# Masked multi-head attention with a pre-norm: own steps for each chunk of products, q and k halves moved one by one, three-term denominators, no loops

## What is computed

```python
h = jnp.maximum(_layernorm(x, axis=-1), 0.0)
q = heads(h @ Wq + bq); k = heads(h @ Wk + bk); v = heads(h @ Wv + bv)
scores = jnp.einsum('bhqd,bhkd->bhqk', q, k) * scale
scores = jnp.where(mask[:, None] == 0, -jnp.inf, scores)
attn = jax.nn.softmax(scores, axis=-1)
out = jnp.einsum('bhqk,bhkd->bhqd', attn, v)
x = x + out.transpose(0, 2, 1, 3).reshape(b, s, D_MODEL) @ Wo + bo
```

## Time and profile before

| | |
|---|---|
| median of three runs | 2085.54 us (2085.31 to 2088.58) |
| the profiled execution | 2085.51 us |
| its span, first to last instruction | 2083.6 us |
| granted TensorE clock, mean | 0.989 |
| PE busy | 1932.5 us, 93% |
| DVE, ACT, POOL busy | 75%, 71%, 62% |
| chain that ended last, PE's share | 76% |
| PE idle before scores, in wait for a mask | 61.4 us |

### The profile page before, as it was taken

How to read it: one execution, slowest core, us unless ns; L and a number is a source line. 1 busy time by engine, 2 the same in 40 slices (tenths; PEclk the granted TensorE clock), 3 DMA queues, 4 the chain that set the end, 5 groups by cost and what they waited for, 6 DMA issues and landing times.

```text
span 2083.6 us, 40441 instructions
## 1 busy us (share of the span) xinstructions
PE 1932.5 (93%) x14336; PEld 776.5 (37%) x14336; DVE 1557.3 (75%) x1587; ACT 1478.1 (71%) x1765; POOL 1302.1 (62%) x581
## 2 busy tenths in 40 slices
PE   3799899998999999999999999999899998999977
PEld 2334344343344333443334333334333343444312
DVE  5688777878768787687867877778767787767773
ACT  3577786677867788668876778767777677866672
POOL 0377567556666567656667557666557566676574
PEclk8999999999999999999999999999999999999999
DMA  5433244342444324343351434424234332442302
GB/s 177 122 87 96 82 112 132 88 107 64 120 112 124 83 76 132 86 122 86 92 142 56 115 93 117 119 74 119 81 109 122 88 106 66 117 122 64 74 1 81
DMA packets 103222, 206.61 MB, mean 99 GB/s; under 512 B 11616, under 2 KB 11744, under 8 KB 103008
## 3 DMA queue, kind: packets, MB, share of 16 engines
q1 hardware_dynamic: 103008, 203.80, 35.2%
HBM read 153.43 MB, written 50.33 MB: 98 GB/s over the span
## 4 chain that ended last, share of the span: by engine, by line
PE 76%; DVE 7%; issue 6%; DMA 5%; ACT 2%; POOL 1%; SPq 1%; DVEq 0%; ACTq 0%; POOLq 0%
PE ps L694 20%; PE ps L681 19%; PE ps L654 15%; PE ps L705 10%; PE ps L668 7%; PE ps L661 6%; DVE ring L905 4%; DMA k_stack<-k_parts 2%; DMA k_parts<-k_part 1%; SPq L513 1%; DMA edges<-adjT 1%; ACT hT_hi L776 1%; DVE k_part L918 1%; POOL acc L1079 1%; ACT ring L770 1%
## 5 line engine op out<-in xcount | busy, mean ns | idle before, releaser
L905 DVE TENSOR_TENSOR ring<-ps,mask 128x1024 f32<-128x1024 f32 x1024 | 1234.6, 1219 | 435.7 <-PE ps L681 399.9
L770 ACT ACTIVATE ring<-ring 128x1024 f32<-128x1024 f32 x1024 | 1069.7, 1051 | 382.9 <-DVE ring L905 374.6
L1079 POOL TENSOR_TENSOR acc<-ring 128x1024 f32<-128x1024 f32 x256 | 604.1, 2371 | 730.2 <-ACT ring L770 729.4
L681 PE MATMUL ps<-q_stack,k_stack 128*128 128x512 f16 x2048 | 610.4, 382 | 85.2 <-DVE ring L905 61.4
L1079 POOL TENSOR_TENSOR acc<-acc,ring 128x1024 f32<-128x1024 f32 x256 | 617.6, 2432 | 0.0
L694 PE MATMUL ps<-ring,v_sb 128*32 128x512 f32 x4096 | 509.1, 604 | 0.0
L681 PEld LDWEIGHTS ps<-q_stack,k_stack 128*128 128x128 f16 x2048 | 157.1, 98 | 481.8 <-DVE ring L905 246.4
L694 PEld LDWEIGHTS ps<-ring,v_sb 128*32 128x32 f32 x4096 | 100.9, 109 | 252.3 <-issue 218.1
L705 PE MATMUL ps<-acc,ones 128*32 128x512 f32 x1024 | 139.8, 597 | 2.7 <-issue 2.6
L705 PE MATMUL ps<-ring,ones 128*32 128x512 f32 x1024 | 137.3, 592 | 0.0
L661 PE MATMUL ps<-wv_hi,hT_hi 128*128 128x128 f16 x1024 | 103.1, 219 | 3.2 <-DVE k_part L918 3.2
(11 more groups left out here) (80 smaller groups left out, 1593.4 us busy)
## 6 DMA issues: line engine op xcount, KB each, us to landing
x_in<-x SPq DMA_DIRECT2D x168, 256.0 KB, 2.7
edges<-adjT SPq DMA_DIRECT2D x128, 256.0 KB, 2.9
q_stack<-q_parts SPq DMA_DIRECT2D x128, 256.0 KB, 4.9
k_stack<-k_parts SPq DMA_DIRECT2D x128, 256.0 KB, 5.0
q_parts<-q_part SPq DMA_DIRECT2D x32, 512.0 KB, 2.7
k_parts<-k_part SPq DMA_DIRECT2D x32, 512.0 KB, 2.9
out<-x_in SPq DMA_DIRECT2D x56, 256.0 KB, 2.1
ring<-x SPq DMA_DIRECT2D x2, 1024.0 KB, 6.6
```

Of the source, the lines that this page charges most:

```text
L681: i = nc.tensor.matmul(ps_s(j)[:, hh, :], stack["k"][:, up % 2, h, kt * P:(kt + 1) * P], stack["q"][:, up % 2, h, half * HALF:(half + 1) * ...
L770: nc.scalar.activation(tile, tile, ACT.Exp, scale=SCALE / UP / UP).then_inc(s["prob_ready"], 1)
L905: nc.vector.tensor_tensor(ring[:, slot_of(kt, pair), :].rearrange("p (a n) -> p a n", n=HALF), ps_s(j), mask[:, kt:kt + 1, half * HALF:(ha ...
L1079: nc.gpsimd.tensor_tensor(acc[:, group, pair, :], first_of, ring[:, slot_of(kt, pair), :], ALU.add).then_inc(s["sum_done"], 1)
```

## The change

- `TERMS = "AB7"`: A is now the sum of kt 0 to 3, B that of kt 4 to 6, and only kt 7 is taken from the ring. POOL makes ten sums a sweep instead of eight. Groups of blocks come after steps 6, 10, 14 and 18, the last with four blocks.
- Every chunk has a window of steps of its own for each of the four units (`PRODUCTS`), and lags of its own for ACT's high half and squares and for DVE's part. The windows are the same in all graphs; chunks that a graph doesn't have leave theirs empty. The chunks t are spread from step 13 of unit 2 to step 13 of unit 3. Statistics, normalisation, masks and POOL's additions of the bias get steps from tables as well.
- Each half (high, low) of q and k is stored by a DMA of its own and loaded by two of the four stack loads when that half is in DRAM. Stores wait one step behind the half, loads three.
- DVE waits for the mask key tile by key tile instead of for eight at once; the output is scaled at step 5 instead of 4.
- The `Fori` loop of each engine is unrolled in Python: all eight graphs stand one after another in the program.

```diff
-BLOCKS = {6: ("p0", "p1"), 10: ("p2", "p3", "dA"), 14: ("p4", "p5"), 16: ("p6", "dB", "d6"), 18: ("p7", "d7")}
-TERMS = "AB67"
+BLOCKS = {6: ("p0", "p1"), 10: ("p2", "p3"), 14: ("p4", "p5", "dA"), 18: ("p6", "dB", "p7", "d7")}
+TERMS = "AB7"
+SUMMED = {1: 0, 2: 2, 3: 4, 5: 6, 6: 8}
+SUMS = 10
+SUMMED_AT = {"A": 6, "B": 10}
+PRODUCTS = [
+    {("q", 0): (0, 3), ("q", 1): (4, 5), ("k", 0): (7, 8), ("k", 1): (8, 11), ("y", 0): (12, 13), ("y", 1): (13, 16), ("v", 0): (16, 19), ("y", 2): (21, 21), ("y", 3): (23, 23), ("y", 4): (25, 27), ("v", 1): (28, 30), ("n", 0): (31, 31)},
+    {("y", 5): (1, 4), ("q", 0): (5, 8), ("y", 6): (9, 9), ("q", 1): (11, 12), ("y", 7): (14, 16), ("k", 0): (16, 21), ("k", 1): (21, 22), ("v", 0): (23, 28), ("v", 1): (29, 31), ("n", 0): (31, 32)},
+    {("q", 0): (1, 4), ("k", 0): (5, 8), ("v", 0): (9, 12), ("t", 0): (13, 13), ("q", 1): (15, 17), ("t", 1): (18, 19), ("k", 1): (20, 23), ("t", 2): (24, 24), ("v", 1): (26, 29), ("t", 3): (29, 30), ("n", 0): (31, 31), ("t", 4): (32, 32)},
+    {("q", 0): (1, 4), ("t", 5): (5, 5), ("k", 0): (6, 7), ("t", 6): (9, 9), ("v", 0): (10, 12), ("t", 7): (12, 13), ("q", 1): (14, 15), ("k", 1): (18, 21), ("v", 1): (22, 27), ("n", 0): (28, 28)},
+]
...
+LOW_AFTER = [
+    {("q", 0): 2, ("q", 1): 2, ("k", 0): 1, ("k", 1): 2, ("y", 0): 1, ("y", 1): 1, ("y", 2): 1, ("y", 3): 1, ("y", 4): 1, ("n", 0): 1},
+    {("y", 5): 4, ("q", 0): 2, ("y", 6): 2, ("q", 1): 1, ("y", 7): 1, ("k", 0): 1, ("k", 1): 2, ("n", 0): 3},
+    {("q", 0): 3, ("k", 0): 3, ("t", 0): 1, ("q", 1): 2, ("t", 1): 2, ("k", 1): 2, ("t", 2): 1, ("t", 3): 2, ("n", 0): 1, ("t", 4): 1},
+    {("q", 0): 1, ("t", 5): 3, ("k", 0): 3, ("t", 6): 1, ("t", 7): 2, ("q", 1): 2, ("k", 1): 2, ("n", 0): 0},
+]
...
+BIAS_AT = {(0, 5): 0, (0, 7): 1, (0, 10): 2, (0, 11): 3, (0, 22): 4, (0, 26): 5, (0, 29): 6, (1, 0): 7}
+RECIPROCAL_AT, SCALE_O_AT = 2, 5
...
-            def store_parts(kind):
-                sp.dma_start(parts[kind], part[kind][:]).then_inc(s[kind + "_stored"], 16)
+            def store_part(kind, hl):
+                sp.dma_start(parts[kind][:, hl, :], part[kind][:, hl, :]).then_inc(s[f"{kind}_{('high', 'low')[hl]}_stored"], 16)
+            def load_stack(U, parity, kind, hl):
+                sp.wait_ge(s[f"{kind}_{('high', 'low')[hl]}_stored"], 16 * (U + 1))
...
+                        for c in [c for c in HIGH_AT.get(G - 1, ()) if c[2] in "qk"]:
+                            if c[3] == 1:
+                                sp.wait_ge(s["high_ready"], chunk_no(SPLIT, c) + 1)
+                                store_part(c[2], 0)
+                        for c in [c for c in LOW_AT.get(G - 1, ()) if c[2] in "qk"]:
+                            if c[3] == 1:
+                                sp.wait_ge(s["low_ready"], chunk_no(SPLIT, c) + 1)
+                                store_part(c[2], 1)
...
-            with pe.Fori(1, B - 1) as b:
+            for b in range(1, B - 1):
...
                 pool.wait_ge(s["prob_ready"], U * TILES + j + 1)
-                if k == 1 and pair == 0 and not very_first:
+                begins = kt % 4 == 1
+                if begins and pair == 0 and not very_first:
                     pool.wait_ge(s["den_done"], len(TERMS) * (V - 1) + group + 1)
-                if k == 2:
-                    pool.wait_ge(s["sum_done"], 8 * V + 4 * group + pair + 1)
+                if not begins:
+                    pool.wait_ge(s["sum_done"], n - 1)
```

More of the change, by code:

```diff
@@ L317, in spread_out @@
-def spread_out(chunks, slots):
-    total = sum(PIECES[kind] * COST[kind] for kind, _ in chunks)
-    plan, spent = {}, 0
-    for kind, t in chunks:
-        for piece in range(PIECES[kind]):
-            runs = plan.setdefault(slots[len(slots) * spent // total], [])
-            if runs and runs[-1][:2] == (kind, t):
-                runs[-1] = (kind, t, runs[-1][2], piece + 1)
-            else:
-                runs.append((kind, t, piece, piece + 1))
-            spent += COST[kind]
-    return plan
@@ L332, in chunk_plan @@
-def chunk_plan(up, first, last):
-    chunks = [c for c in chunk_list(up, first, last) if c != NORMS]
-    if not chunks:
-        return {}
-    plan = spread_out([c for c in chunks if c[0] != "t"], SLOTS_OF[up])
-    plan.update({at: [("t", t, 0, PIECES["t"])] for (u, at), t in T_AT.items() if u == up and ("t", t) in chunks})
-    return {**plan, NORMS_AT[up]: [(*NORMS, 0, PIECES["n"])]}
-def chunk_ends(up, first, last):
-    return {(kind, t): at for at, runs in chunk_plan(up, first, last).items() for kind, t, _, to in runs if to == PIECES[kind]}
@@ new lines, in chunk_plan @@
+def chunk_plan():
+    plan = {}
+    for b in range(B):
+        for up in range(UNITS):
+            for (kind, t), (a, z) in PRODUCTS[up].items():
+                if kind == "y" and b == 0 or b == B - 1 and (kind == "t" or up == UNITS - 1):
+                    continue
+                slots = [j for j in range(a, z + 1) if j % SWEEP not in BUSY] or [a]
+                for at, run in spread_out((b, up, kind, t), [(b * UNITS + up) * TILES + j for j in slots]).items():
+                    plan.setdefault(at, []).append(run)
+    return plan
@@ L561, in graph @@
+                        for g, u, kind, t in [c for c in HIGH_AT.get(G - 3, ()) if c[2] in "qk"]:
                             if t == 1:
-                                sp.wait_ge(s["low_ready"], chunk_no(SPLIT, b, up, first, (kind, t)) + 1)
-                                store_parts(kind)
-                        for kind, t in ending_at(up, first, last, j - 4, "y"):
-                            sp.wait_ge(stored[t % X_SLOTS], 16 * ((b - 1) * (QT // X_SLOTS) + t // X_SLOTS + 1))
+                                load_stack(unit_no(g, u) + 1, (u + 1) % 2, kind, 0)
@@ L566, in graph @@
+                        for g, _, kind, t in [c for c in LOW_AT.get(G - 3, ()) if c[2] == "y"]:
+                            sp.wait_ge(stored[t % X_SLOTS], 16 * ((g - 1) * (QT // X_SLOTS) + t // X_SLOTS + 1))
                             if t + X_SLOTS < QT:
[L567 removed]
+                                load_x(g - 1, t + X_SLOTS)
                             elif not last:
[L569 to L570 removed]
+                                load_x(g + 1, t + X_SLOTS - QT)
@@ L718, in graph @@
                     U = unit_no(b, up)
-                    plan = chunk_plan(up, first, last)
                     for j in range(TILES):
@@ L730, in graph @@
                         blocks(U, up, half, r, first and up == 0 and half == 0)
-                        for kind, t, piece, to in plan.get(j, ()):
-                            chunk(b, up, first, kind, t, piece, to)
+                        for run in PLAN.get(U * TILES + j, ()):
+                            chunk(*run)
             pe.wait_ge(s["const_loaded"], 16 * 6)
@@ L879, in _ @@
             graph(0, True, False)
-            with act.Fori(1, B - 1) as b:
+            for b in range(1, B - 1):
                 graph(b, False, False)
@@ L1040, in _ @@
             graph(0, True, False)
-            with dve.Fori(1, B - 1) as b:
+            for b in range(1, B - 1):
                 graph(b, False, False)
@@ L1104, in _ @@
             graph(0, True, False)
-            with pool.Fori(1, B - 1) as b:
+            for b in range(1, B - 1):
                 graph(b, False, False)
```

227 lines of the change are left out of this document (103 added, 124 removed), and 8 rows, old and new, of tables (HIGH_AFTER, SQUARE_AFTER).

## The result

The changed kernel takes 1982.16 us (median of four executions, 1979.96 to 1990.77) against 2086.53 us for the kernel before on the same chip: a ratio of 0.9506, 95% interval 0.948 to 0.9533. The forecast was 1983 us, the range 1953 to 2025. The total came out as forecast; several of its terms did not, the six inner graphs and the end of the program above all, and they cancelled.

The account below looks back on a forecast made before the run. PE, busy for 93% of the span, was taken as the bound. Six inner graphs 88.1 us less, graph 0 6.5, graph 7 7.1, prologue 1: 2085.5 - 102.7 = 1983 us, range 1953 to 2025.

Parts of the forecast that it names:

- (a): In each sweep, three terms drop one block and one passage: 1.09 us a sweep, 69.8 us less for 64 sweeps.
- (b): POOL's two more sums a sweep, hidden with 0 to 2 us to spare; only the last unit becomes POOL's, 52.4 us.
- (c): Chunks in windows of their own: PE loses 5.5 instead of 7.6 us a graph in light steps, 2.1 us less.
- The floor by the masks of the light steps: Three steps between block groups, paced by masks: 3.1 us, plus 0.6 to 1.8 us per further DVE instruction.
- The windows level nothing: Rival: only (a) and (e) act, 2085.5 - 69.8 - 17.4 = 1998 us; within the forecast's 62%.
- (e): Straight code ends PE's stall behind the jump back at the start of five graphs: 17.4 us less.
- (d): Halves of q and k moved one by one hide the k chain: 0.6 us less a graph, 1 us in the prologue.
- DVE and POOL block each other: Rival: low halves of o last up to 2.2 us longer beside POOL: 20 us more, 2003 us; within the 62%.
- POOL's chain decides: Rival: tile 3 comes 1 us later, five of eight sweeps a graph wait for term B: 2023 us; 20%.
- k late at the end of unit 2: Rival: PE waits there for k, 1.3 us in eight graphs: 1994 us; within the forecast's 62%.
- Fewer waits than by the floor: Rival: of 94 us left as PE's waits, a third may go where steps are even: 1953 us; 14%.
- Slower by fetch stalls: Rival: straight code stalls PE about 4 us a time; at one a sweep 2240 us; half of 4%.

Follow-up runs that it names:

- experiment 5: The changed kernel with four terms and eight POOL sums a sweep again, all else kept: 2045.44 us, ratio 0.9793.
- experiments 9 and 10: 9: changed kernel with four edge slots and k1 of unit 3 two steps earlier, 1979.39 us. 10: changed kernel, POOL one addition a sweep more, 2003.83 us.
- the copy: The changed kernel run again without any change, as the base for its variants: 1980.99 us, ratio 0.95.
- experiment 11: The changed kernel with POOL adding only the first 512 columns of each sum (wrong denominators for every second head): 1970.72 us, ratio 0.9442.
- experiment 4: The kernel before with loops written out and three terms, chunks spread and halves moved as before: 2042.89 us, ratio 0.9793.
- experiment 6: The changed kernel with both halves of q or k stored by one 512 KB DMA, then four loads: 2005.49 us, ratio 0.9608.
- experiment 3: The kernel before with loops written out and DVE's low half of o in unit 2 one step later: 2066.1 us, ratio 0.9899.
- experiments 2 and 3: 2: kernel before with its loops written out, 2077.25 us. 3: the same, low half of o in unit 2 one step later, 2066.1 us.
- experiment 7: The changed kernel with k1 of unit 3 two steps earlier (16 to 19) and v1 at steps 20 to 27: 1994.35 us, ratio 0.9542.

## Why the prediction was right, and where it wasn't

**(a) Three terms.** Right in size where it can act: 64.5 us in experiment 5 for 69.8. PE's busy time fell by 70.2 us in all. Wrong as a term on its own: with the old spreading 23 us.

**(b) POOL.** "Hidden with 0 to 2 us to spare" held in the graphs. PE itself waited for acc for 5.3 us, its weight loads for 19.1, under the 20 I had named; experiments 9 and 10 show how near the edge is. The step that failed is the last sweep. I took the last unit as POOL's, at 52.4 us for 50.4, and added 2 us. The two sweeps were that fast or faster, but the sum stopped at the unit's end and did not follow the last sums out of it: there nothing hides them. PE's pause of 4.93 us and the low clock (some 4 us in the copy, where the three groups behind this pause and three of the output run at 1.9 us instead of 1.04, against two of the output before) make 9 of the +9.8. It is an error of 8 us; experiment 11 shows its cause, since there the pause and the slow groups right behind it are gone and the stretch takes 42.9 us. I never wrote down what the path behind the last score pair is.

**(c) Windows.** The floor by the masks of the light steps was the right rule: unit 2 takes 54.8 us (54 to 56 forecast), graph 7's 53.9 (53.9), graph 0's first two units got longer, as forecast, to 114.0 (112.5). Their split was luck: the forecast had the larger loss, 5.8 us, in unit 1, which stayed at 55.0; unit 0 grew by 3.5 us, and PE's waits for a mask in it from 4.1 to 8.1. Unit 1, at 58.5 us, is under the 60 to 62 I had set: of the 2.4 us that the floor gave it, PE is idle for 0.6. The total rested on comparing two end states, and there the floor was applied to both. The mistake is in the rival *The windows level nothing*: I gave it (a) and (e) in full, 1998 us, though my own floor says that PE work taken from light steps comes back as waiting. Measured: 2043 us in experiment 4. From there the windows, without the halves, bring 37 us (experiment 6), not the 2.1 a graph that I had written beside (c).

**(d) Halves.** The chain was hidden at the end of unit 2, as taken: no wait there. But the same chain at the end of unit 3 was not looked at: I followed SP past its two new waits and said that the edges' loads behind them have several steps, and did not turn it round. It is k's store that stands behind an edges' load which waits for ACT. It costs unit 3 0.8 us a graph in the copy and 1.0 in the profile of the result, and unit 3 is the only one of an inner graph that got longer (57.3 us for 56.4). Its PE work fell by only 0.3 us: (a) takes 2.2 out, but eight more transposes and sixteen more products for the norms now fall into it. The price of (d) itself, 0.6 us a graph, was read off the kernel before, where k had its old place. With the new windows it is 3 us a graph. The Trainium skill's rule that I had set against this part (SBUF — State Buffer, "The DMA setup-cost knee": each transfer pays about 2 us, so for DMA-bound transfers move much at a time) would have had whole stores no worse. The runs go the other way by 24.5 us: here PE waits for a chain of two transfers, and half of it can leave before the low half is made. Whether the smaller store or the two loads that go ahead bring it was not separated.

**(e) Loops.** Right: 20 us in experiment 3 for 17.4, and no inner graph of the copy is longer than another by over 1.5 us (234.1 to 235.6). The profile of before alone could not show that DVE and POOL shut each other out in another way with it.

**The six inner graphs** came out 10 us better than forecast, 234.7 us each for 236.4. PE's busy time fell by 10.1 us a graph, not 8.7, and it idles for 4.7. That is 1.27 us a sweep instead of 1.09: 0.12 of it went with the loops (experiment 3 has 1435.0 us of busy PE in graphs 1 to 6, the kernel before 1440.9), so that (a) and the windows have 1.15; where the last 0.06 come from stays open. This and the end of the program cancelled; the total was right partly by luck.

**The rivals.** *DVE and POOL block each other*: real, in a form I had not priced. I spread 20 us over all low halves; in the copy the median low half is 1.39 us and PE sees next to nothing of it, in the profiled execution one of 32 took 8.64 us, and that is the 8.3 us by which its unit 2 is long. The page I had cited (the Trainium skill, SBUF — State Buffer, "SBUF: two separate sides") says that who starts first gets the shared port for the whole instruction; experiments 2 and 3 agree, with 0.07 us between the two outcomes. It has nothing on a second instruction of the same engine following on; the row of 674.72 shows DVE shut out across several. *POOL's chain decides*: no, but by 1 us in unit 0 as soon as k is on time. *k late at the end of unit 2*: no; at the end of unit 3. *Fewer waits than by the floor*: a part of it, PE idles for 4.7 us in an inner graph where the floor left 5.5. The 1890 us of PE work in that rival don't follow from the earlier trace rows: 1932.5 less 69.8 is 1863, and the two profiles have 1862.3 and 1859.2. *Slower by fetch stalls*: none; 35,056 instructions in a row, and unit 0 is the same in each inner graph within 0.4 us. The Trainium skill (Runtime: NRT & Kernel Launch, "Instruction fetch mechanics") says that a taken branch breaks the sequential prefetch; experiment 3 puts 4 us on one jump back of this kernel.

## What to carry to other kernels

Where PE alternates between heavy and light steps, work taken off it is worth its time only if the remaining products are spread so that no run of light steps falls under the pace of the masks: price the two edits together, as two end states, never one by one. Follow every chain that you lengthen out of the last unit to the end of the program, since there the cover is gone, and here the pause of 4.93 us cost the clock as well. When a wait is taken away, look for the next chain with the same deadline, and for what the moved transfers are now in front of: twice here the gain went to a neighbour (edges, POOL's sums).

## What the hardware did that was not expected

- An instruction of DVE with two SBUF inputs was shut out for 8.64 us, behind sums of POOL that follow without a gap, once in 32 (and in none of the other profiled executions of the changed kernel or its variants, where the longest is 3.4 us). Which of the two engines loses can turn on 0.07 us, so that an edit elsewhere (loops written out) costs 1.5 us a unit by it.
- A pause of 2.7 us in the last unit, while PE stands for a mask, is followed by the low clock in some executions and not in others: in the profile of the result 0.53 over the next 6.75 us behind 2.70 us, and the unit took 50.9 us; in the copy 1.00 over 6.72 us behind 2.71, and 49.0. It fell there in six of the eight profiled executions of the changed kernel and its variants with a pause of 2.70 to 2.72 us at this place.
- After a pause of 4.93 us PE's granted clock was 0.50 for the next 3.4 us of its work, and after a further pause of 4.62 us 0.51 over 5.05 us, then 1.00. Before the change only the second pause was there: 4.60 us, and behind it 0.54 over 3.1 us.
- In the changed kernel a load of 256 KB lands in 2.8 us at the median of x and in 4.9 of the k stack; where stack and edges were fetched together, single loads took 7.27 us (the stack, changed kernel) and 7.39 (the edges, experiment 7).
